# Graph attention and product-key attention in one kernel: another order of work in the prologue

## The reference, cut to what matters

```python
# x: (8, 1024, 128); adj: (1024, 1024) int32, 1 where there is an edge
x = x + gnn(layernorm(x), adj, W, a)
x = x + ffn(layernorm(x), Wq_pk, pk_keys, Wq, keys_table, values_table, Wo)

def gnn(h, adj, W, a):
    Wh = h @ W
    e = Wh @ a[:D] + swap(Wh @ a[D:])          # source term + destination term
    e = where(e > 0, e, 0.2 * e)
    e = where(adj > 0, e, -inf)
    return elu(softmax(e) @ Wh)                # the neighbour sum

def ffn(x, ...):                               # x as (2, 512)-like batches, 8 heads
    q = (x @ Wq) * 128 ** -0.5
    sim = (x @ Wq_pk) . pk_keys                # two halves of 128 keys per head
    scores, ind = top 16 of sums of the two halves' top 16     # softmax over them
    k = sum over 16 of scores * keys_table[ind]
    v = sum over 16 of scores * values_table[ind]
    return causal_attention(q, k, v) @ Wo
```

## Time and profile before

| | us |
|---|---|
| median of 3 runs | 10367.11 (10366.17 to 10372.42) |
| the profiled execution | 10365.63 |
| its span | 10363.8 |
| mean granted TensorE clock | 0.748 |

### The profile page before, as it was taken

One profiled execution on the slowest core, in us unless ns is written; L12 is line 12 of the kernel. 1 busy time (PEld: TensorE's weight loads), 2 busy tenths in 40 slices (PEclk: granted clock), 3 DMA queues, 4 the chain that ended last, 5 costly groups with the idle time before them and its releaser, 6 DMA issues.

```text
span 10363.8 us, 122720 instructions
## 1 busy us (share of the span) xinstructions
PE 5475.3 (53%) x23108; PEld 4290.3 (41%) x23108; DVE 6960.2 (67%) x42588; ACT 2991.5 (29%) x9770; POOL 7776.4 (75%) x8209
## 2 busy tenths in 40 slices
PE   5655555555555555555555555555555555555455
PEld 4444444444444444444444444444444444434333
DVE  8866666666666666666666666666666666666663
ACT  4322232222322223222232222322223222222222
POOL 5777777777777777777777777777777777777776
PEclk7777777777777777777777777777777777777777
DMA  3333333333333333333333333333333333333333
GB/s 110 101 105 105 105 109 105 105 105 105 109 105 105 105 105 109 105 105 105 106 108 105 105 105 108 106 105 105 105 108 105 105 105 105 106 106 105 105 105 97
DMA packets 414093, 1093.52 MB, mean 106 GB/s; under 512 B 132480, under 2 KB 150144, under 8 KB 413440
## 3 DMA queue, kind: packets, MB, share of 16 engines
q0 software_dynamic: 393216, 1074.27, 36.0%
q1 hardware_dynamic: 20352, 14.82, 0.5%
HBM read 1084.36 MB, written 4.19 MB: 105 GB/s over the span
## 4 chain that ended last, share of the span: by engine, by line
POOL 74%; issue 24%; DVE 1%; PE 1%; POOLq 0%; DMA 0%; ACT 0%; SPq 0%; DVEq 0%; ACTq 0%
POOL ring L278 74%; DVE hot L896 0%; DMA wo<-in_Wo 0%; POOLq L293 0%; PE ps_w L558 0%; POOLq L291 0%; PE ps_o L611 0%; PE ps_s L635 0%; POOLq L292 0%; DVE nmax L943 0%; DMA ring<-in_table,idx 0%; POOLq L289 0%; PE ps_p L497 0%; DVE sidx L844 0%; DVE sidx L850 0%
## 5 line engine op out<-in xcount | busy, mean ns | idle before, releaser
L278 POOL DMA_INDIRECT ring<-in_table,idx x8192 | 7774.9, 949 | 2561.2 <-issue 2494.5
L558 PE MATMUL ps_w<-ring,diag 128*128 128x256 f32 x8192 | 2974.1, 542 | 4259.2 <-DMA ring<-in_table,idx 4259.2
L558 PEld LDWEIGHTS ps_w<-ring,diag 128*128 128x128 f32 x8192 | 2293.2, 287 | 4838.1 <-issue 4257.9
L815 DVE TENSOR_SCALAR ps_v<-ring,wgt 128x256 f32<-128x256 f32 x512 | 248.8, 486 | 2105.2 <-DMA ring<-in_table,idx 2105.2
L896 DVE SCALAR_TENSOR_TENSOR hot<-rank,posf,cand 128x54 f32<-128x54 f32 x8192 | 1659.5, 271 | 0.3
L385 ACT COPY probT<-ps_p 128x512 f32<-128x512 f32 (+3 forms) x768 | 342.4, 480 | 4065.1 <-PE ps_p L602 4064.9
L818 DVE SCALAR_TENSOR_TENSOR ps_v<-ring,wgt,ps_v 128x256 f32<-128x256 f32 x3072 | 1477.4, 481 | 19.6
L368 ACT ACTIVATE diag<-ident,wgt 128x128 f32<-128x128 f32 x4096 | 1253.3, 395 | 1.5 <-PE ps_w L558 1.5
L377 ACT ACTIVATE prob<-ps_s,nmax 128x128 f32<-128x128 f32 (+7 forms) x512 | 378.9, 740 | 1986.2 <-DVE nmax L943 1986.2
L829 DVE TENSOR_TENSOR kv<-part,ps_w 128x256 f32<-128x256 f32 x512 | 215.8, 421 | 819.7 <-PE ps_w L558 470.9
L611 PE MATMUL ps_o<-probT,kv 128*128 128x128 f32 x4608 | 633.9, 284 | 52.2 <-ACT probT L385 49.1
(11 more groups left out here) (117 smaller groups left out, 7017.1 us busy)
## 6 DMA issues: line engine op xcount, KB each, us to landing
ring<-in_table,idx POOLq DMA_INDIRECT x8192
xin<-in_x SPq DMA_DIRECT2D x8, 512.0 KB, 4.9
mask<-in_adj SPq DMA_DIRECT2D x1, 4096.0 KB, 13.8
out_x<-acc SPq DMA_DIRECT2D x64, 64.0 KB
ring<-in_WqpkT SPq DMA_DIRECT2D x1, 512.0 KB, 15.9
ring<-in_keysT SPq DMA_DIRECT2D x1, 512.0 KB, 17.9
wq<-in_Wq SPq DMA_DIRECT2D x1, 512.0 KB, 18.3
wo<-in_Wo SPq DMA_DIRECT2D x1, 512.0 KB, 19.3
```

Source lines behind the costliest of these rows:

```text
L278: pool.indirect_dma_start(out=ring[:, t % RING, k, :], out_offset=None, in_=table, in_offset=bass.IndirectOffsetOnAxis(ap=idx[:, t, k:k + ...
L558: ins = nc.tensor.matmul(pw_ps, diag[:, k, :], ring[:, t % RING, k, :], start=(k == 0), stop=(k == PE_ROWS - 1))
```

## The change

No instruction of the graph layer or of the choice is removed. The adjacency is loaded as row tile 0 and, behind `WqpkT` and `keysT`, row tiles 1 to 7. `projection(0)` makes the product of row tile 0 first (into `wh_ps`), then the two destination products (into `ps_s`), then the other seven. The edges run two row tiles ahead of the rest, and the mask of a row tile is made right in front of its edges. The key products stand behind the first neighbour sum, and their copies behind the second row of exponentials. `graph_recip` is the reciprocal taken out of `graph_elu`.

```diff
 # SyncE
-            sp.dma_start(mask[:].bitcast(I32), adj.rearrange("(t p) n -> p t n", p=P)).then_inc(adj_dma, 16)
-            sp.dma_start(wpk_t, WqpkT).then_inc(in_dma, 16)
-            sp.dma_start(keys_t, keysT).then_inc(in_dma, 16)
+            sp.dma_start(mask[:, 0, :].bitcast(I32), adj[0:P, :]).then_inc(adj_dma, 16)
+            sp.dma_start(wpk_t, WqpkT).then_inc(pk_dma, 16)
+            sp.dma_start(keys_t, keysT).then_inc(pk_dma, 16)
+            sp.dma_start(mask[:, 1:TILES, :].bitcast(I32), adj[P:N, :].rearrange("(t p) n -> p t n", p=P)) \
+                .then_inc(adj_rest_dma, 16)
 # ScalarE, projection
-                for t in range(TILES):
+                opening = isinstance(bn, int) and bn == 0
+                if opening:
+                    act.wait_ge(wh_mm, 1)
+                    nc.scalar.copy(wh[:, 0, :], wh_ps).then_inc(wh_copied, 1)
+                    for c in range(2):
+                        act.wait_ge(dst_mm, c + 1)
+                        nc.scalar.copy(dst[:, c * 512:(c + 1) * 512], ps_s[:, c * 512:(c + 1) * 512]) \
+                            .then_inc(dst_copied, 1)
+                for t in range(1 if opening else 0, TILES):
...
 # ScalarE, prologue
+            graph_exp(0)
+            graph_copy(0)
+            graph_exp(1)
             for g in range(4):
                 act.wait_ge(pk_mm, g + 1)
...
-            act.wait_ge(in_dma, 4 * 16)
+            act.wait_ge(in_dma, 2 * 16)
             nc.scalar.copy(wq_cur[:], wq[:, 0, :]).then_inc(wq_copied, 1)
-            graph_exp(0)
-            graph_copy(0)
...
                 if it < TILES - 1:
-                    graph_exp(it + 1)
                     graph_copy(it + 1)
                 choose_softmax(it)
+                if it < TILES - 2:
+                    graph_exp(it + 2)
 # TensorE, projection
+                if opening:
+                    nc.tensor.matmul(wh_ps, hnT[:, 0:P], w_ext[:], start=True, stop=True).then_inc(wh_mm, 1)
+                    for c in range(2):
+                        nc.tensor.matmul(ps_s[:, c * 512:(c + 1) * 512], w_dst[:], hnT[:, c * 512:(c + 1) * 512],
+                                         start=True, stop=True).then_inc(dst_mm, 1)
...
 # TensorE, prologue
-            pe.wait_ge(in_dma, 4 * 16)
+            graph_transposes(0)
+            graph_sum(0, 0, wh_ps)
+            pe.wait_ge(pk_dma, 2 * 16)
+            pe.wait_ge(dst_copied, 2)
             for g in range(4):
...
-            pe.wait_ge(dst_copied, 2)
-            graph_transposes(0)
-            graph_sum(0, 0, ps_s)
+            graph_transposes(1)
...
                 if it < TILES - 1:
-                    graph_transposes(it + 1)
                     graph_sum(0, it + 1, ps_s)
+                if it < TILES - 2:
+                    graph_transposes(it + 2)
 # VectorE
+            def graph_recip(g):
+                dve.wait_ge(g_exp, g + 1)
+                after(step(nc.vector.reciprocal(row[:, R_RECIP:R_RECIP + 1], row[:, R_SUM:R_SUM + 1])))
...
             dve.wait_ge(adj_dma, 16)
-            for t in range(TILES):
-                c = step(nc.vector.tensor_scalar(mask[:, t, :], mask[:, t, :].bitcast(I32), 0, -BIG,
-                                                 ALU.is_le, ALU.mult))
-            after(c)
+            after(open_mask(0))
             graph_edges(0, 0, 0)
+            dve.wait_ge(adj_rest_dma, 16)
+            after(open_mask(1))
+            graph_recip(0)
+            graph_edges(0, 1, 1)
             for it in range(TILES):
-                graph_elu(it, it, ps_s)
+                graph_elu(it, it, ps_s if it else wh_ps)
                 graph_out(0, it, it, True)
                 graph_norm(it)
-                if it < TILES - 1:
-                    graph_edges(0, it + 1, it + 1)
                 c = choose_sets(0, it, it)
...
                 choose_rows(it, it, c)
+                if it < TILES - 1:
+                    graph_recip(it + 1)
+                if it < TILES - 2:
+                    after(open_mask(it + 2))
+                    graph_edges(0, it + 2, it + 2)
                 weights(it, it)
```

More of the change, by code:

```diff
@@ L136, in gat_and_product_key_attention @@
         adj_dma = sem("adj_dma")
+        adj_rest_dma = sem("adj_rest_dma")
+        pk_dma = sem("pk_dma")
         x_dma = sem("x_dma")
@@ L304, in projection @@
                     nc.scalar.copy(hnT[:, c * 512:(c + 1) * 512], ps_p[:, c, :]).then_inc(hnT_copied, 1)
-                for t in range(TILES):
+                opening = isinstance(bn, int) and bn == 0
[7 more added lines that the diff above has]
+                for t in range(1 if opening else 0, TILES):
                     act.wait_ge(wh_mm, TILES * bn + t + 1)
                     nc.scalar.copy(wh[:, t, :], ps_p[:, t % 2, 0:P + 1]).then_inc(wh_copied, 1)
-                for c in range(2):
-                    act.wait_ge(dst_mm, 2 * bn + c + 1)
-                    nc.scalar.copy(dst[:, c * 512:(c + 1) * 512], ps_p[:, c, :]).then_inc(dst_copied, 1)
+                if not opening:
+                    for c in range(2):
+                        act.wait_ge(dst_mm, 2 * bn + c + 1)
+                        nc.scalar.copy(dst[:, c * 512:(c + 1) * 512], ps_p[:, c, :]).then_inc(dst_copied, 1)
             def graph_exp(g):
@@ L492, in projection @@
                     pe.wait_ge(aux_copied, 2)
-                for t in range(TILES):
-                    if t >= 2:
+                opening = isinstance(bn, int) and bn == 0
+                if opening:
+                    nc.tensor.matmul(wh_ps, hnT[:, 0:P], w_ext[:], start=True, stop=True).then_inc(wh_mm, 1)
+                    for c in range(2):
+                        nc.tensor.matmul(ps_s[:, c * 512:(c + 1) * 512], w_dst[:], hnT[:, c * 512:(c + 1) * 512],
+                                         start=True, stop=True).then_inc(dst_mm, 1)
+                for t in range(1 if opening else 0, TILES):
+                    if t >= (3 if opening else 2):
                         pe.wait_ge(wh_copied, TILES * bn + t - 1)
@@ L499, in projection @@
                 pe.wait_ge(wh_copied, TILES * (bn + 1))
-                for c in range(2):
+                for c in range(0 if opening else 2):
                     nc.tensor.matmul(ps_p[:, c, :], w_dst[:], hnT[:, c * 512:(c + 1) * 512],
@@ L748, in graph_edges @@
                 dve.wait_ge(dst_copied, 2 * bn + 2)
+                if isinstance(bn, int) and bn == 0:
+                    dve.wait_ge(wh_copied, it + 1)
                 dve.wait_ge(g_exp, g)
@@ L916, in _, with open_mask @@
             projection(0)
+            def open_mask(t):
+                return step(nc.vector.tensor_scalar(mask[:, t, :], mask[:, t, :].bitcast(I32), 0, -BIG,
+                                                    ALU.is_le, ALU.mult))
             dve.wait_ge(adj_dma, 16)
-            for t in range(TILES):
-                c = step(nc.vector.tensor_scalar(mask[:, t, :], mask[:, t, :].bitcast(I32), 0, -BIG,
-                                                 ALU.is_le, ALU.mult))
-            after(c)
+            after(open_mask(0))
             graph_edges(0, 0, 0)
+            dve.wait_ge(adj_rest_dma, 16)
+            after(open_mask(1))
+            graph_recip(0)
+            graph_edges(0, 1, 1)
             for it in range(TILES):
-                graph_elu(it, it, ps_s)
+                graph_elu(it, it, ps_s if it else wh_ps)
                 graph_out(0, it, it, True)
                 graph_norm(it)
-                if it < TILES - 1:
-                    graph_edges(0, it + 1, it + 1)
                 c = choose_sets(0, it, it)
@@ L993, in head @@
                         if t == 3:
+                            graph_recip(g)
                             graph_elu(h, g, wh_ps)
```

2 lines of the change are left out of this document (removed).

## The result

| | before | after |
|---|---|---|
| median of 11 runs each, in turn on one chip | 10369.21 (10365.25 to 10372.78) | 10390.53 (10388.14 to 10397.01) |
| the profiled execution | 10365.63 | 10388.14 |
| its span | 10363.8 | 10386.3 |
| its mean granted TensorE clock | 0.748 | 0.75 |

The ratio after to before is 1.0022, with a 95% interval of 1.0013 to 1.0031: slower by 21.3 us, or 0.21%. That is just over the 0.2% that a measurement of this kernel can tell from no change. 10392.5 us was forecast, 10383 to 10399.

A forecast was written before the change was run, and what follows sets the result against it. The run was taken to move with the prologue's eighth index set, through POOL's wait for unit 6's row sum: opening -5.7 us plus loop +31.3 gave +25.6 us, forecast 10392.5 us, range 10383 to 10399.

The forecast's parts named there:

- The loop: VectorE from first to eighth index set: 4.1 + 16.7 + 13.6 - 3.1 = +31.3 us on 133.55.
- Masks: VectorE's loop: masks of units 2 to 7 move in, 0.68 us each, 4.1 us in all.
- Bare similarities: VectorE's loop: edges no longer cover the wait before the choice; 2.79 us in 6 intervals, 16.7 us.
- ELU behind exp and diagonals: Loop: ScalarE's late row exp and eight diagonals delay the ELU that VectorE needs; 13.6 us.
- Stalls: Loop: VectorE's waits for rows of unit 5 and TensorE's work on gathered rows go; -3.1 us.
- The opening: Before the loop: first exp 10.8 us earlier, ELU 3.8 earlier, first index set 5.7 us earlier, at 51.5.
- rival B: Opening: TensorE at its upper clock; key products alone give back 3.2 us (10389.3), all 5.8 (10386.7); 20 in 100.
- Its second part: Opening: unit 0's neighbour sum (1.7 us) and its transposes (0.9) also at TensorE's upper clock.
- the likeliest case: Whole run: opening -5.7 us and loop +31.3, giving 10392.5 us; 60 in 100.
- The table's price: ScalarE's exp table load: 1.28 us per switch; the skill's 1.38 us drain would make the sum +27.0.
- Rival D: Loop: VectorE waits some 1 us for TensorE's weighing in each of six iterations; +31.6, 10398.5 us; 12 in 100.
- E: Opening no shorter, as the adjacency's rest or copies in ScalarE's queue end late; +31.3, 10398 us; 3 in 100.

The follow-up runs named there:

- masks in the opening: Changed kernel with the masks of units 2 to 7 moved from the loop into VectorE's wait for the first ELU; 10387.33 us, 1.002 to the kernel before.
- The second experiment: Changed kernel with ScalarE making the diagonals of unit it-1 before the exponentials of row tile it+2, not behind them; 10382.47 us, 1.0011 to the kernel before.
- the third experiment: Changed kernel with mask and edges of it+2 back between normalisation and choice, their exponentials before the softmax one; 10367.44 us, 0.9998 to the kernel before.

## Why the prediction was right, and where it was not

**What bounds the run: right.** The two waits of POOL are where the time went, and they grew by 22.3 us for a span that grew by 22.5. In every row of the table with a span, gathers, issue and waits make the span less 27.6 to 28.6 us.

**The loop: right, +31.35 for +31.3.** It took 164.90 us, and 164.91 with the old opening. The terms:
- Masks: 4.45 measured (masks in the opening), 4.1 forecast.
- Bare similarities: eight waits, 21.9 us; without the first one's 2.75 these are 19.2, where 2.59 had stood. That is 16.6 for a forecast of 16.7.
- ELU behind exp and diagonals: seven waits, 19.3 - 4.1 = 15.2 us in all, where seven of 0.25 to 0.33 had been 1.8. That is 13.4 for 13.6. The second experiment gives the diagonals' share, 11.6; 5 x 2.43 = 12.2 us of diagonals were to be had.
- Stalls: those of the earlier trace rows are gone. No wait for gathered rows is left in the changed loop.
- That all hang on the place of the edges and their exp, the third experiment shows: 30.2 of the 31.3 went with it.

**The opening: right up to the key products, then mis-sized.** The first exp came at 22.79 (22.9 forecast), the neighbour sum at 30.65 (30.9). The term that was wrong is the 7.73 us from the start of the key products to ScalarE's next instruction. It took 35.14 - 30.54 = 4.60, since the products ran at 2.4 GHz in the profiled execution; VectorE's wait for the first ELU was 4.1 us and not 7. So 48.30 stands where 51.5 was forecast, 3.2 us earlier, the price given to rival B's first part. Its second part, the transposes and the neighbour sum at the upper clock, did not come (0.50 and 0.51). B with the products alone gives 10389.3, and the likeliest case gives 10392.5; the median lies between, 1.2 and 2.0 from them. But both stand on a median of 10367.11 for the kernel before, which took 10369.21 beside the changed one. As differences, +21.3 was measured for +22.2 of B's first part and +25.4 of the likeliest case. The gathers' own scatter is a few us too, so the median alone decides nothing; the rows do. The price was right, and 20 in 100 was too low: the products ran mostly at the upper clock in nine of eleven executions. The sign given for B, a first gather below 48, was set for the whole of B and did not show (48.76).

One thing was missed and made good by another. VectorE waited for `w_ext` until 6.28, and in the kernels with one load of the adjacency until 5.27 to 5.76. The whole opening began some 0.8 us late. But the projection behind the destination products was quicker than forecast: the last `wh` copy ended at 20.72 and not at 21.6, and VectorE's edges were what the exp waited for last, 0.77 us behind the table load.

**The table's price: the row was right.** The load at 20.73 was through at 22.01 and VectorE's edges came last; the load at 32.40 in the earlier trace rows was followed by its exp after 1.29. The drain that the Trainium skill (ScalarE: Activation LUTs, What ACT_TABLE_LOAD costs) puts behind a load would have made the exp start at 20.73 + 1.28 + 1.38 = 23.39; it started at 22.79, so the trace does not agree.

**The clock.** The rows first: idle for 3.76 us, then 0.50 through 6.4 us of transposes and neighbour sum, then 1.00. The Trainium skill (TensorE: Matmul & The Clock Gate, The HAM clock gate) has activity release the clock, and here the trace agrees. In two other executions the same work in the same place did not raise it. There TensorE had been idle for 3.45 and 3.51 us before the transposes, and for 3.75 to 3.77 in the nine others; whether that is the reason is not shown. One reading of the prediction was too coarse: before, the key products did not run at 0.50 throughout. They began at 1.00, and the clock was down 0.5 us later, at 25.2. So the argument against B was weaker than it looked: the clock fell inside that work and did not come back in the 6.4 us left of it.

**POOL: right.** Five waits of about 5 us were forecast: 4.72 and 5.05 or 5.06 were measured. The last wait was 17.38 for 16. Rival D, a wait for TensorE's weighing, did not come. E (no shorter opening) did not either: the rest of the adjacency landed at 22.8, just in time, and its mask started at 22.80 without a wait. (With the edges in the cover it landed at 24.4, and the mask waited 0.46 us.)

## What to carry to other kernels

Find the one event through which a prologue reaches the bounding queue, and price every move by how it shifts that event. Here an opening shortened by 8.9 us was worth 8.9, and a loop lengthened by 31.3 cost 31.3, whatever the busy shares said. Work that is independent of a wait is worth most when it stands in front of that wait: the same edges, moved from before the similarities to behind the indices, cost 30 us with all that follows them. And when work is moved late on one engine, read what is queued behind its consumer on the next one: eight diagonals behind a late exp, five times over, were 11.6 us. A wait need not carry its name: 4 us of waiting for a row sum stood under "issue".

## What the runs showed of the hardware

- **The same matmuls in the same place ran at either clock.** The 32 key products behind the first neighbour sum took 3.88 to 4.33 us in 9 profiled executions of 11 and 7.19 in two. In their old place, behind 2.89, 3.03 and 3.76 us without a matmul, they took 6.89 to 7.19 in 3 of 3, though they ran for that long without a gap. Why the two differ is open.
- **The small load of `w_ext` landed later in the kernels that load the adjacency in two:** 2.9 to 3.4 us after its issue with one load (three kernels), 3.5 to 4.7 with two (eleven, with the one in which the larger loads were held back at 3.6). The cause was not settled.
- **The gathers' busy time differs from one execution to the next:** 7774.2 to 7782.3 us for 8192 of them, and about 7800 in two executions (the third chip left out). These few us are as large as what one edit here is worth, so edits were judged by events up to 320 us and by POOL's waits.
- **One chip took 13185 us for the kernel that takes 10367 on others,** with VectorE standing still for up to 5.8 us at a time in a choice, and no releaser that the profile names. Why is open.
